# Second layer: the low parts of the turned tiles move from GpSimd to VectorE

## Chip, cores and metric

One NeuronCore of a Trainium2 chip runs the whole kernel in one launch. The metric is device time in microseconds (us), lower is better. Engines in the rows: PE is TensorE, PEld its weight loads, DVE VectorE, ACT ScalarE, POOL GpSimd, SP SyncE (it starts the transfers). PSUM is the memory that PE writes to, SBUF the one that all engines work from.

## What is computed

Two layers over x of shape 8 x 512 x 32 x 32, that is 8 batches of 512 channels by 1024 tokens, all in float32:

```python
# layer 0: group norm, 8 heads of full attention over 1024 tokens, projection, residual
# layer 1 (the change is in here):
q, kk, v = (einsum('oc,bcn->bon', w, xf) for w in (wq, wk, wv))
importance = sum(xf * xf, axis=1)
_, topk_idx = top_k(importance, 256)                 # 256 tokens of each batch
q_sel, k_sel, v_sel = those columns of q, kk, v
q_sel, k_sel = layer_norm(q_sel), layer_norm(k_sel)
attended = softmax(clip(q_sel @ k_sel.T * scale, -80, 80)) @ v_sel
out = v.at[chosen tokens].set(attended)
return x + einsum('oc,bcn->bon', wo, out)
```

## The kernel before

PE multiplies float32 data as pairs: each operand is split into a high part (a copy rounded to the fp32r type) and a low part (the value minus its high part), and a product is high x high + high x low + low x high. So every tile that PE is to read must first be split, one engine writing the high part and another the low one.

The first layer fills the span up to about 2300 us and is not touched. The second handles a batch in four phases, and a *round* i works on four batches at once: t = i + 2 is turned to tokens, its importances are formed and its 256 tokens counted out; a = i + 1 has its chosen rows gathered; b = i is projected to q and k, normed, and attends; c = i - 1 is read back from memory, where the attended rows have been written among its tokens, is turned back to channels and multiplied by the output weights. Only rounds 1 to 8 have a c. In rounds 6 and 7 there is no t any more, in round 8 only c is left. `round_order` (L1104) gives PE's order in a round:

```python
order = [("q", b), ("t", 0, t), ("t", 1, t), ("k", b), ("t", 2, t), ("t", 3, t), ("x", 0, c), ("x", 1, c),
         ("qt", b), ("kt", b), ("rows", t), ("x", 2, c), ("x", 3, c), ("xs", a), ("s", b), ("e", 0, c),
         ("e", 1, c), ("at", b), ("e", 2, c), ("u", b), ("id", t), ("e", 3, c)]
```

`t`: tokens turned (L1281). `q`, `k`: projections (L1356). `x`: a tile of c turned back, 8 transposes into 128 x 1024 of PSUM (L1291). `qt`, `kt`, `xs`: normed q, normed k and the chosen rows turned (L1332). `rows`: importances spread (L1315). `s`: top scores (L1367). `e`: an output tile, 24 matmuls; the first one needs all four split tiles x, a quarter of its matmuls each (L1306). `u`: attended rows (L1389). `id`: sum of the chosen numbers (L1324).

Each of these units writes one of four PSUM slots, dealt out ahead by `tile_slots`. Before PE writes a slot, `free` (L1234) waits for the last reader of the unit that held it. In rounds 2 to 5 `rows` follows x 0 in its slot, x 2 follows x 1, x 3 follows `qt`, `xs` follows `kt`, and `s` follows x 2. In round 8 each e follows the x of its number.

ScalarE goes through the same order: for a turned tile x, `turned_back` (L1458) makes a full float32 copy in SBUF (L1463) and the high part (L1464). GpSimd's `x_low` (L1769) subtracts the two, in SBUF, for all four tiles of the round (L1773); it cannot read PSUM. For `qt`, `kt` and `xs` ScalarE writes the high part (L1485) and VectorE the low one straight from PSUM (`low`, L1600).

VectorE's order in a round stands in the loop at L1689: last output tile of the batch before, layer norm of q and of k (L1607 to L1618), `guard` of the importances, low parts of qt and kt, counts 0 and 1, low part of xs, softmax, counts 2 to 7 among two output tiles, and `choose` (L1564), on whose flags `id` waits. A *count* compares the 1024 importances with 128 of them (L1547, L1549, L1551).

The full copy had no place of its own: its buffer is given up as soon as it is named, and x_low lies on the same addresses, so GpSimd subtracts in place.

Of the kernel before, what the change touches and what calls it, by code (L numbers as in the profile page):

```python
# [8 lines left out]
ALU = mybir.AluOpType  # L9
ACT = mybir.ActivationFunctionType  # L10
F32 = mybir.dt.float32
# [3 lines left out]
P = 128  # L15
# [1078 lines left out]
def batches_of(i):  # L1094


    return [batch(b) for b in (i + 2, i + 1, i, i - 1)]
# [46 lines left out]
def top_layer(nc, x1, y, raw4, ln_wb, shapes_only, ident):  # L1144
# [3 lines left out]
    with first.ctx as ctx:  # L1148
# [3 lines left out]
        def sem(name):  # L1152
            return ctx.enter_context(nc.semaphore(name))
# [30 lines left out]
        fin = flat(qn)[:, 0:RT * TOP].bitcast(U32).rearrange("p (r c) -> p r c", r=RT)  # L1184
        xsel = sb("x_chosen", [P, RT, C])
        xh = sb("x_high", [P, CT, N], F32R)
        with nc.sbuf_tensor("x_back_full", [P, CT, N], F32) as xf:
            pass
        xl = sb("x_low", [P, CT, N], F32R)
        ranks, lower = sb("rank_numbers", [P, TOP]), sb("lower_tokens", [P, P])  # L1190
        equal = sb("equal_flags", [P, P])[:, :].bitcast(BF16).rearrange("p (i x) -> p i x", i=2)
# [8 lines left out]
        xtok = [nc.dram_tensor(f"token_major{i}", [N, C], F32).ap() for i in range(4)]  # L1200

        s_unit, s_load_w = sem("s_unit1"), sem("s_load_w")
        a_tok, a_sq, a_hi, a_ex, a_xf, a_xh, a_row, a_z = (
            sem(n) for n in ("a_tok", "a_sq", "a_hi", "a_ex", "a_xf", "a_xh", "a_row", "a_z"))
        d_imp, d_cnt, d_sel, d_id, d_lo, d_ln, d_sm, d_set, d_row, d_y = (
            sem(n) for n in ("d_imp", "d_cnt", "d_sel", "d_id", "d_lo", "d_ln", "d_sm", "d_set", "d_row", "d_y"))
        p_pow, p_xl = sem("p_pow"), sem("p_xl")
        a_w, d_w, s_wr, a_wqk, p_wqk, s_lnb = (
            sem(n) for n in ("a_w", "d_w", "s_wr", "a_wqk", "p_wqk", "s_lnb"))
        s_gath = [sem(f"s_gath{r}") for r in range(RT)]  # L1210
# [17 lines left out]
        def slot(u):  # L1228
            return ring[:, SLOT1[u], :]

        def second_tensor(pe, last_output):
            mm, tr = nc.tensor.matmul, nc.tensor.transpose

            def free(u):  # L1234

                w = HOLDER1[u]
                if w is None:
                    if SLOT1[u] < 2:
                        pe.wait_ge(told["s_p32"], TILES)
                    elif SLOT1[u] == 2:  # L1240
                        pe.wait_ge(told["s_mx"], 2 * NT * ALL_HEADS)
                        pe.wait_ge(told["s_nd"], 2 * ALL_HEADS)
                    else:
                        pe.wait_ge(told["s_kql"], told["units_read"][0])
                        pe.wait_ge(told["s_vl"], told["units_read"][1])
                else:
                    b = w[-1]
                    if w[0] == "t":
                        pe.wait_ge(a_sq, NT * b + 2 * w[1] + 2)
                    elif w[0] == "w":  # L1250
                        pe.wait_ge(d_w, w[1] + 1)
                    elif w[0] == "o":
                        pe.wait_ge(told["s_x1"], told["residual_done"](w[1]))
                    elif w[0] == "rows":
                        pe.wait_ge(d_cnt, cn((("c", NT - 1), b)))
                    elif w[0] == "id":
                        pe.wait_ge(d_id, ids((1, b)))
                    elif w[0] == "x":
                        pe.wait_ge(a_xh, CT * b + w[1] + 1)
                    elif w[0] == "e":  # L1260
                        pe.wait_ge(d_y, CT * b + w[1] + 1)
                    elif w[0] == "u":
                        pe.wait_ge(a_z, b + 1)
                    elif w[0] in ("q", "k"):
                        pe.wait_ge(d_ln, ln((w[0], "w1", b)))
                    elif w[0] == "s":
                        pe.wait_ge(d_sm, sf(("scale", b)))
                    else:
                        pe.wait_ge(d_lo, lo(w))
                return slot(u)  # L1270
# [24 lines left out]
            def output(u):  # L1295
                _, t, b = u
                out = free(u)
                pe.wait_ge(a_w, 2)
                pe.wait_ge(d_w, 2)
                for c in range(CT):  # L1300
                    if t == 0:
                        pe.wait_ge(a_xh, CT * b + c + 1)
                        pe.wait_ge(p_xl, CT * b + c + 1)
                    for i, (a, w) in enumerate(((0, xh), (0, xl), (1, xh))):
                        for n in range(2):
                            done = mm(out[:, n * HALF:(n + 1) * HALF], ww[a][:, c, t * P:(t + 1) * P],  # L1306
                                      w[:, c, n * HALF:(n + 1) * HALF], start=(c == 0 and i == 0),
                                      stop=(c == CT - 1 and i == 2))
                done.then_inc(s_unit, 1)
# [126 lines left out]
        def second_scalar(act, last_o_high):  # L1436
# [21 lines left out]
            def turned_back(u):  # L1458
                _, c, b = u
                act.wait_ge(s_unit, unit(u))  # L1460
                if b > 0:
                    act.wait_ge(s_unit, unit(("e", CT - 1, b - 1)))
                act_(xf[:, c, :], slot(u), ACT.Copy).then_inc(a_xf, 1)  # L1463
                act_(xh[:, c, :], slot(u), ACT.Copy).then_inc(a_xh, 1)  # L1464

            def rows_high(b):
# [57 lines left out]
        def second_vector(dve, last_o_low, last_residual):  # L1524
# [56 lines left out]
            def rows_low(b):  # L1581
                dve.wait_ge(a_row, b + 1)
                v.tensor_tensor(flat(xrow[1][:, :, :]), flat(xsel[:, :, :]), flat(xrow[0][:, :, :]).bitcast(F32),
                                ALU.subtract).then_inc(d_row, 1)

            def y_tile(t, b):
                u, m = ("e", t, b), CT * b + t
                dve.wait_ge(s_unit, unit(u))
                dve.wait_ge(s_again[t % 2], 16 * (2 * b + t // 2 + 1))
                if m > 1:  # L1590
                    dve.wait_ge(s_out[m % 2], 16 * (m // 2))
                else:
                    for c in range(CT):
                        dve.wait_ge(*told["stored"](BATCH - 1, c))
                v.tensor_tensor(ys[:, m % 2, :], slot(u), xr[:, t % 2, :], ALU.add).then_inc(d_y, 1)
# [93 lines left out]
            for i in ROUNDS[2:]:  # L1689
# [14 lines left out]
                    layer_norm("k", b)  # L1704
                if t is not None:
                    guard(t)
                if b is not None and i > 0:
                    low(("qt", b))
                    low(("kt", b))
                if t is not None:  # L1710
                    for n in range(2):
                        count(t, n)
                if a is not None:
                    low(("xs", a))
                if b is not None:
# [24 lines left out]
        def second_gpsimd(pool):  # L1740
# [25 lines left out]
                    nc.gpsimd.indirect_dma_start(xtok[b % 4], bass.IndirectOffsetOnAxis(idx[:, b % 3, r:r + 1], 0),  # L1766
                                                 changed[b % 2][:, r, :], None).then_inc(s_scat[r], 16)

            def x_low(b):  # L1769
                for c in range(CT):  # L1770
                    pool.wait_ge(a_xf, CT * b + c + 1)
                    pool.wait_ge(a_xh, CT * b + c + 1)
                    nc.gpsimd.tensor_tensor(xl[:, c, :], xf[:, c, :], xh[:, c, :].bitcast(F32),  # L1773
                                            ALU.subtract).then_inc(p_xl, 1)

            def weights_low(i):
                row = (wq_row, wk_row)[i]
                pool.wait_ge(a_wqk, i + 1)
# [4 lines left out]
            weights_low(0)  # L1783
            weights_low(1)
            for i in ROUNDS:
                _, a, b, c = batches_of(i)
                if a is not None:
                    gather(a)
                if i == -1:
                    rstd("q", a)  # L1790
                    rstd("k", a)
                elif b is not None and i > 0:
                    rstd("q", b)
                    rstd("k", b)
                if c is not None:
                    x_low(c)
                if b is not None:
                    scatter(b)

# [201 lines left out]
```

## Time and profile before

| | |
|---|---|
| median of 3 runs | 2801.49 us (2796.53 to 2802.63) |
| profiled execution, its own time | 2800.42 us |
| its span | 2798.7 us |
| PE busy | 2640.9 us, 94% |
| VectorE busy | 2068.8 us, 74% |
| ScalarE busy | 1599.2 us, 57% |
| GpSimd busy | 318.9 us, 11% |
| granted clock of PE, mean | 0.984 |

The share of busy time is a mean over the whole program. The round lengths, from one projection of q to the next, are about 56 us in rounds 2 to 5, 54 in round 6, 52 in round 7 and 44 for the rest. "Idle before" in a row of the timeline is the time for which the engine stood still before the instruction, with the one that released it.

### The profile page before, as it was taken

The page shows a single profiled execution, that of the slowest core. Times are in us where ns is not written, and L with a number is a line of the kernel's source. Part 1 is how long each engine was busy: PE and PEld are TensorE (multiplying, and loading weights), DVE is VectorE, ACT ScalarE, POOL GpSimd, SP SyncE. Part 2 cuts the span into 40 slices and gives each one's busy share as a digit, 9 for nine tenths or more (in the row PEclk, how much of TensorE's full clock was granted, in tenths as well). Part 3 has the DMA queues.
Part 4 walks back from the last instruction along what each step waited for, and adds up shares of the span by engine and source line. Part 5 has one row for each costly group of instructions (what it writes and reads, how often), then busy time and mean ns, then how long its engine had stood idle before and what let it go on. Part 6 is the DMA issues. An engine that isn't in the chain of part 4 may idle for free.

```text
span 2798.7 us, 33246 instructions
## 1 busy us (share of the span) xinstructions
PE 2640.9 (94%) x11856; PEld 2195.8 (78%) x11856; DVE 2068.8 (74%) x3262; ACT 1599.2 (57%) x1962; POOL 318.9 (11%) x166
## 2 busy tenths in 40 slices
PE   6999999999999999999999999999999975899987
PEld 5778887888888888888888888888888764787776
DVE  6888768876887688778877887788777756677652
ACT  3767646764676467646755675567556732533331
POOL 1001001000000000000000000001000121322222
PEclk9999999999999999999999999999999997999999
DMA  4522241214122312131213221322222253645534
GB/s 159 169 57 76 56 126 47 80 54 125 50 76 62 120 46 87 54 117 49 85 53 117 57 79 51 119 56 80 65 83 80 75 211 139 222 166 203 192 110 143
DMA packets 154850, 279.48 MB, mean 100 GB/s; under 512 B 51776, under 2 KB 52032, under 8 KB 154176
## 3 DMA queue, kind: packets, MB, share of 16 engines
q1 hardware_dynamic: 152128, 268.98, 30.5%
q0 software_dynamic: 2560, 8.39, 0.9%
q8 instruction: 96, 1.57, 0.2%
q14 instruction: 66, 0.54, 0.1%
HBM read 180.04 MB, written 63.18 MB: 87 GB/s over the span
## 4 chain that ended last, share of the span: by engine, by line
PE 76%; DVE 15%; issue 3%; ACT 3%; DMA 2%; SPq 1%; POOL 0%; POOLq 0%; DVEq 0%; ACTq 0%
PE tiles L371 8%; PE tiles L372 8%; PE tiles L373 8%; PE tiles L427 8%; PE tiles L473 7%; PE tiles L450 7%; PE tiles L467 7%; PE tiles L466 7%; PE tiles L446 7%; DVE p_low L695 4%; PE tiles L1306 3%; PE tiles L1356 3%; DVE row_max L679 2%; DVE flags L1547 1%; DVE flags L1549 1%
## 5 line engine op out<-in xcount | busy, mean ns | idle before, releaser
L679 DVE TENSOR_REDUCE row_max<-tiles 128x1 f32<-128x512 f32 x1014 | 695.1, 686 | 421.2 <-PE tiles L427 416.6
L543 ACT ACTIVATE p_high<-tiles 128x1024 fp32r<-128x1024 f32 x512 | 525.8, 1027 | 616.7 <-PE tiles L450 615.9
L695 DVE TENSOR_TENSOR p_low<-p_full,p_high 128x1024 fp32r<-128x1024 f32 x512 | 663.1, 1295 | 6.0 <-ACT p_full L546 5.2
L546 ACT ACTIVATE p_full<-tiles 128x1024 f32<-128x1024 f32 x512 | 521.8, 1019 | 0.0
L427 PE MATMUL tiles<-k_high_low,q_high_high 128*128 128x512 f32 x1014 | 409.9, 404 | 7.6 <-DVE row_max L679 6.9
L466 PE MATMUL tiles<-p_high,v_high 128*128 128x512 f32 x1024 | 406.9, 397 | 2.2 <-ACT num_den L562 1.3
L467 PE MATMUL tiles<-p_high,v_low 128*128 128x512 f32 x1024 | 402.5, 393 | 0.0
L878 POOL TENSOR_TENSOR o_normed<-num_den,o_normed 64x1024 f32<-64x1024 f32 x64 | 165.4, 2584 | 2050.8 <-DMA o_normed<-rec_rows 2050.8
L427 PEld LDWEIGHTS tiles<-k_high_low,q_high_high 128*128 128x128 f32 x1014 | 313.1, 309 | 63.3 <-DVE row_max L679 21.7
L473 PE MATMUL tiles<-p_low,v_high 128*128 128x512 f32 x1024 | 326.5, 401 | 16.1 <-DVE p_low L695 15.7
L450 PE MATMUL tiles<-q_low_max,k_high_one 65*128 65x512 f32 x1024 | 325.6, 399 | 1.0 <-DMA q_low_max<-row_max_top 1.0
L371 PE MATMUL tiles<-h_high,w_high 128*128 128x512 f32 x768 | 305.2, 397 | 18.6 <-DVE row_max L679 9.3
L446 PE MATMUL tiles<-q_high_high,k_high_low 128*128 128x512 f32 x1024 | 317.2, 391 | 0.0
L372 PE MATMUL tiles<-h_low,w_high 128*128 128x512 f32 x768 | 302.1, 393 | 0.0
L373 PE MATMUL tiles<-h_high,w_low 128*128 128x512 f32 x768 | 300.9, 392 | 0.0
L446 PEld LDWEIGHTS tiles<-q_high_high,k_high_low 128*128 128x128 f32 x1024 | 192.4, 188 | 47.0
L450 PEld LDWEIGHTS tiles<-q_low_max,k_high_one 65*128 65x128 f32 x1024 | 193.8, 190 | 43.5 <-DMA q_low_max<-row_max_top 2.0
L473 PEld LDWEIGHTS tiles<-p_low,v_high 128*128 128x128 f32 x1024 | 190.1, 189 | 47.3 <-DVE p_low L695 27.8
L466 PEld LDWEIGHTS tiles<-p_high,v_high 128*128 128x128 f32 x1024 | 192.9, 188 | 38.2 <-ACT num_den L562 2.1
L467 PEld LDWEIGHTS tiles<-p_high,v_low 128*128 128x128 f32 x1024 | 192.6, 188 | 38.0
L371 PEld LDWEIGHTS tiles<-h_high,w_high 128*128 128x128 f32 x768 | 146.1, 190 | 45.0 <-issue 25.2
L373 PEld LDWEIGHTS tiles<-h_high,w_low 128*128 128x128 f32 x768 | 145.4, 189 | 32.3
(168 smaller groups left out, 3259.7 us busy)
## 6 DMA issues: line engine op xcount, KB each, us to landing
x_tiles<-in_x SPq DMA_DIRECT2D x64, 512.0 KB, 5.3
w_high<-w_split SPq DMA_DIRECT2D x126, 256.0 KB, 2.8
w_low<-w_split SPq DMA_DIRECT2D x126, 256.0 KB, 2.9
k_high_one<-k_high_low SPq DMA_DIRECT2D x128, 128.0 KB, 2.3
q_high_high<-q_high_high SPq DMA_DIRECT2D x128, 128.0 KB, 2.3
o_normed<-rec_rows SPq DMA_DIRECT2D x64, 256.0 KB, 3.7
x<-x_tiles SPq DMA_DIRECT2D x32, 512.0 KB, 4.0
x_full<-x SPq DMA_DIRECT2D x32, 512.0 KB, 6.0
```

What stands on the lines that cost most here:

```text
L371: mm(fill[:, :], w1, high[:, c, cols], start=(c == 0), stop=False)
L372: mm(fill[:, :], w1, low[:, c, cols], start=False, stop=False)
L373: last = mm(fill[:, :], w2, high[:, c, cols], start=False, stop=(c == CT - 1))
L427: mm(max_bank(h, i, n)[:, :], q1[:, q_slot(h), first:first + HALF - 3:4], k1[:, k_slot(h), n * HALF:(n + 1) * HALF], start=True, stop=True ...
L446: mm(out[:, n * HALF:(n + 1) * HALF], k1[:, wk, keys[n]], q1[:, wq, queries], start=True, stop=False)
L450: last = mm(out[:, n * HALF:(n + 1) * HALF], k2[0:HD + 1, wk, keys[n]], q2[0:HD + 1, wq, queries], start=False, stop=True)
L466: mm(pv[:, :], weights_of(v1, t, n), p, start=(t % 4 == 0 and n == 0), stop=False)
L467: last = mm(pv[:, :], weights_of(v2, t, n), p, start=False, stop=False)
L473: last = mm(pv[:, :], weights_of(v1, t, n), pl[:, t % 2, n * HALF:(n + 1) * HALF], start=False, stop=(t % 4 == 3 and n == 1))
L543: nc.scalar.activation(ph[:, r, :], ring[:, r, :], ACT.Exp, scale=ATT_SCALE).then_inc(s_ph, 1)
L679: nc.vector.reduce_max(mcol[:, h % 2, n, i:i + 1], max_bank(h, i, n)[:, :], AX_X).then_inc(s_mx, 1)
L695: tt(pl[:, r, :], p32[:, r, :], ph[:, r, :].bitcast(F32), ALU.subtract).then_inc(s_pl, 1)
```

## The change

VectorE takes the low part of each turned tile from its PSUM slot, as it does for q, k and the chosen rows. ScalarE writes only the high part, GpSimd has no part in it, and the full copy goes. A slot with a turned tile is now free when its low part is done, not when its high part is. In VectorE's order the first two low parts stand ahead of those of q and k, the other two between counts 0 and 1.

```diff
@@ top_layer, allocation and semaphores
         xh = sb("x_high", [P, CT, N], F32R)
-        with nc.sbuf_tensor("x_back_full", [P, CT, N], F32) as xf:
-            pass
         xl = sb("x_low", [P, CT, N], F32R)
...
-        a_tok, a_sq, a_hi, a_ex, a_xf, a_xh, a_row, a_z = (
-            sem(n) for n in ("a_tok", "a_sq", "a_hi", "a_ex", "a_xf", "a_xh", "a_row", "a_z"))
+        a_tok, a_sq, a_hi, a_ex, a_xh, a_row, a_z = (
+            sem(n) for n in ("a_tok", "a_sq", "a_hi", "a_ex", "a_xh", "a_row", "a_z"))
...
-        p_pow, p_xl = sem("p_pow"), sem("p_xl")
+        p_pow, d_xl = sem("p_pow"), sem("d_xl")
@@ second_tensor, free
                     elif w[0] == "x":
-                        pe.wait_ge(a_xh, CT * b + w[1] + 1)
+                        pe.wait_ge(d_xl, CT * b + w[1] + 1)
@@ second_tensor, output
                     if t == 0:
                         pe.wait_ge(a_xh, CT * b + c + 1)
-                        pe.wait_ge(p_xl, CT * b + c + 1)
+                        pe.wait_ge(d_xl, CT * b + c + 1)
@@ second_scalar, turned_back
-                act_(xf[:, c, :], slot(u), ACT.Copy).then_inc(a_xf, 1)
                 act_(xh[:, c, :], slot(u), ACT.Copy).then_inc(a_xh, 1)
@@ second_vector
+            def x_low(c, b):
+                dve.wait_ge(a_xh, CT * b + c + 1)
+                v.tensor_tensor(xl[:, c, :], slot(("x", c, b)), xh[:, c, :].bitcast(F32), ALU.subtract).then_inc(d_xl, 1)
...
                 if t is not None:
                     guard(t)
+                if c is not None:
+                    x_low(0, c)
+                    x_low(1, c)
                 if b is not None and i > 0:
                     low(("qt", b))
                     low(("kt", b))
                 if t is not None:
-                    for n in range(2):
-                        count(t, n)
+                    count(t, 0)
+                if c is not None:
+                    x_low(2, c)
+                    x_low(3, c)
+                if t is not None:
+                    count(t, 1)
                 if a is not None:
                     low(("xs", a))
@@ second_gpsimd
-            def x_low(b):
-                for c in range(CT):
-                    pool.wait_ge(a_xf, CT * b + c + 1)
-                    pool.wait_ge(a_xh, CT * b + c + 1)
-                    nc.gpsimd.tensor_tensor(xl[:, c, :], xf[:, c, :], xh[:, c, :].bitcast(F32),
-                                            ALU.subtract).then_inc(p_xl, 1)
...
-                _, a, b, c = batches_of(i)
+                _, a, b, _ = batches_of(i)
...
-                if c is not None:
-                    x_low(c)
                 if b is not None:
                     scatter(b)
```

VectorE in round 2 (the same in 1 to 5), from the end of `guard` to the low part of the chosen rows; before:

```order
L1536 COPY_PREDICATED importance<-importance_finite,importance 128x8
L1600 TENSOR_TENSOR q_turned_parts<-tiles,q_turned_parts 128x1024
L1600 TENSOR_TENSOR k_turned_parts<-tiles,k_turned_parts 128x1024
L1549 TENSOR_SCALAR flags,counts<-tiles,importance 128x1024
L1551 SCALAR_TENSOR_TENSOR equal_flags,counts<-tiles,importance,lower_tokens 128x128
L1547 TENSOR_SCALAR flags,counts<-tiles,importance 128x128
L1549 TENSOR_SCALAR flags,counts<-tiles,importance 128x896
L1551 SCALAR_TENSOR_TENSOR equal_flags,counts<-tiles,importance,lower_tokens 128x128
L1600 TENSOR_TENSOR x_chosen_parts<-tiles,x_chosen_parts 128x1024
```

and now, where L1585 is `x_low`, L1601 `low`, and L1544 to L1548 are the counts:

```order
L1533 COPY_PREDICATED importance<-importance_finite,importance 128x8
L1585 TENSOR_TENSOR x_low<-tiles,x_high 128x1024 x2
L1601 TENSOR_TENSOR q_turned_parts<-tiles,q_turned_parts 128x1024
L1601 TENSOR_TENSOR k_turned_parts<-tiles,k_turned_parts 128x1024
L1546 TENSOR_SCALAR flags,counts<-tiles,importance 128x1024
L1548 SCALAR_TENSOR_TENSOR equal_flags,counts<-tiles,importance,lower_tokens 128x128
L1585 TENSOR_TENSOR x_low<-tiles,x_high 128x1024 x2
L1544 TENSOR_SCALAR flags,counts<-tiles,importance 128x128
L1546 TENSOR_SCALAR flags,counts<-tiles,importance 128x896
L1548 SCALAR_TENSOR_TENSOR equal_flags,counts<-tiles,importance,lower_tokens 128x128
L1601 TENSOR_TENSOR x_chosen_parts<-tiles,x_chosen_parts 128x1024
```

Two passes over 128 x 1024 have come in ahead of the low parts of q and k, and two ahead of the second count.

ScalarE in the same place, its order from the last tile turned to tokens on; before:

```order
L1463 ACTIVATE x_back_full<-tiles 128x1024
L1464 ACTIVATE x_high<-tiles 128x1024
L1463 ACTIVATE x_back_full<-tiles 128x1024
L1464 ACTIVATE x_high<-tiles 128x1024
L1485 ACTIVATE q_turned_parts<-tiles 128x1024
L1485 ACTIVATE k_turned_parts<-tiles 128x1024
L1463 ACTIVATE x_back_full<-tiles 128x1024
L1464 ACTIVATE x_high<-tiles 128x1024
L1463 ACTIVATE x_back_full<-tiles 128x1024
L1464 ACTIVATE x_high<-tiles 128x1024
L1485 ACTIVATE x_chosen_parts<-tiles 128x1024
```

and now:

```order
L1461 ACTIVATE x_high<-tiles 128x1024 x2
L1482 ACTIVATE q_turned_parts<-tiles 128x1024
L1482 ACTIVATE k_turned_parts<-tiles 128x1024
L1461 ACTIVATE x_high<-tiles 128x1024 x2
L1482 ACTIVATE x_chosen_parts<-tiles 128x1024
```

Four passes over 128 x 1024 have gone; the high parts stand in the same order as before. On GpSimd the only thing gone from a round is x_low, which stood between the powers of the layer norm and the scatter.

## Rows read from the trace of the kernel before

**Rows 1.** Waits between engines, 2370 to 2799 us: engine line waited for: us, times, longest
```profile
PE tiles L1324 <- DVE chosen L1564: 2.7, 5, 0.7
```
**Rows 2.** Chain of waits, round 4: start us, us, what
```profile
2563.61 0.92 ACT x_chosen_parts L1485
...
2564.56 1.23 DVE x_chosen_parts L1600
...
2586.91 5.59 PE tiles L1306 x24
```
**Rows 3.** Timeline of ACT, round 4: start us, us, operation xcount [idle before <-releaser]
```profile
2554.37 1.01 ACT L1463 ACTIVATE x_back_full<-tiles 128x1024 f32<-128x1024 f32 x1
2555.28 1.02 ACT L1464 ACTIVATE x_high<-tiles 128x1024 fp32r<-128x1024 f32 x1
```
**Rows 4.** Timeline of DVE, round 4
```profile
2554.90 0.17 DVE L1536 COPY_PREDICATED importance<-importance_finite,importance 128x8 f32<-128x8 uint32 x1
2559.07 1.23 DVE L1600 TENSOR_TENSOR q_turned_parts<-tiles,q_turned_parts 128x1024 fp32r<-128x1024 f32 x1 [4.01 <-ACT q_turned_parts L1485]
...
2561.35 1.27 DVE L1549 TENSOR_SCALAR_CACHE_REDUCE flags<-tiles,importance 128x1024 bf16<-128x1024 f32 x1
...
2562.82 0.34 DVE L1547 TENSOR_SCALAR_CACHE_REDUCE flags<-tiles,importance 128x128 bf16<-128x128 f32 x1
...
2564.43 0.08 DVE L1551 DVE_READ_ACCUMULATOR equal_flags<-tiles,importance,lower_tokens 128x1 f32 x1
...
2565.70 0.68 DVE L1625 TENSOR_SCALAR q_k_normed<-tiles 128x512 f32<-128x512 f32 x1
```
**Rows 5.** Timeline of PE, round 4: top scores, and the sum of the chosen numbers
```profile
2562.40 3.12 PE L1367 MATMUL tiles<-k_turned_parts,q_turned_parts 128*128 128x256 f32 x24
...
2585.72 1.19 PE L1324 MATMUL tiles<-chosen,token_numbers 128*128 128x256 f32 x8 [0.64 <-DVE chosen L1564]
```
**Rows 6.** Timeline of DVE, round 1; then the line L1627, all: ns min/median/max
```profile
2388.76 1.22 DVE L1600 TENSOR_TENSOR q_turned_parts<-tiles,q_turned_parts 128x1024 fp32r<-128x1024 f32 x1 [4.01 <-ACT q_turned_parts L1485]
...
2394.66 1.22 DVE L1600 TENSOR_TENSOR x_chosen_parts<-tiles,x_chosen_parts 128x1024 fp32r<-128x1024 f32 x1 [0.47 <-ACT x_chosen_parts L1485]
...
2396.52 0.83 DVE L1627 TENSOR_SCALAR q_k_normed<-q_k_normed 128x512 uint32<-128x512 f32 x1
...
L1627 DVE TENSOR_SCALAR q_k_normed<-q_k_normed x8: 426/548/2214, 2345.9 to 2730.4; 128x512 uint32<-128x512 f32 x8
```
**Rows 7.** Windows, in round 3 and round 4 whole: PE, PEld, DVE, ACT, POOL busy, PEclk, DMA
```profile
2503.00:2508.00 5.00, 4.86 (x28) 4.86 (x29) 4.30 (x12) 4.42 (x5) 4.03 (x3) 0.66 0.26 104
...
2536.00:2592.00 56.00, 51.69 (x289) 43.65 (x288) 39.93 (x107) 22.76 (x38) 15.53 (x11) 1.00 0.59 206
```
**Rows 8.** Round 6: timelines of DVE, POOL and PE, in this order
```profile
2657.74 0.75 DVE L1618 SCALAR_TENSOR_TENSOR q_k_normed<-q_k_normed,ln_rstd,ln_weight_bias 128x512 f32<-128x512 f32 x1
...
2663.36 2.11 DVE L1618 SCALAR_TENSOR_TENSOR q_k_normed<-q_k_normed,ln_rstd,ln_weight_bias 128x512 f32<-128x512 f32 x1
...
2662.57 5.10 POOL L1773 TENSOR_TENSOR x_low<-x_back_full,x_high 128x1024 fp32r<-128x1024 f32 x2
...
2668.28 1.97 PE L1332 MATMUL tiles<-identity,q_k_normed 128*128 128x128 f32 x8 [6.08 <-DVE q_k_normed L1618]
...
2674.41 3.11 PE L1367 MATMUL tiles<-k_turned_parts,q_turned_parts 128*128 128x256 f32 x24
```
**Rows 9.** Round 7: timeline of PE
```profile
2722.10 1.97 PE L1332 MATMUL tiles<-identity,q_k_normed 128*128 128x128 f32 x8 [6.07 <-DVE q_k_normed L1618]
...
2726.53 3.11 PE L1367 MATMUL tiles<-k_turned_parts,q_turned_parts 128*128 128x256 f32 x24 [0.20 <-DVE k_turned_parts L1600]
```
**Rows 10.** Round 8: timelines of POOL and PE
```profile
2766.85 9.37 POOL L1773 TENSOR_TENSOR x_low<-x_back_full,x_high 128x1024 fp32r<-128x1024 f32 x4 [14.01 <-ACT x_high L1464]
...
2769.43 0.70 PE L1306 MATMUL tiles<-x_high,w_part 128*128 128x512 f32 x2
...
2776.36 0.70 PE L1306 MATMUL tiles<-x_high,w_part 128*128 128x512 f32 x2 [0.74 <-POOL x_low L1773]
```

## The prediction

> **What bounds the kernel now.** The change touches only the second layer's rounds 1 to 8, the last 420 us of the span. I read them in this order: the waits between engines, the chain of waits of one round, then the timelines of the engines at the places where the edits stand.
>
> Two kinds of stop lie on the path. PE's sum of the chosen numbers waits for VectorE's flags in each of five rounds [rows 1], 0.64 us in round 4 [rows 5]: once the turned tiles are split, VectorE paces rounds 1 to 5. And twice PE stands 6.1 us for VectorE's layer norm of k, in rounds 6 and 7 [rows 8, 9].
>
> The chain of round 4 [rows 2] shows who paces the stretch before. ScalarE is on it until 2564.53, with its copy of the chosen rows; VectorE starts their low part at 2564.56 and from there to the flags it has no idle time worth naming. Ahead of that VectorE had stood 4.01 us for ScalarE [rows 4]. So in rounds 1 to 5 ScalarE's four full copies lie on the path, and VectorE has a hole about as large as the work that it is to get.
>
> **The change, part by part.**
>
> *Full copies gone (ScalarE).* 32 copies go, four to a round; ScalarE starts one every 0.91 us [rows 3], so 3.6 us a round.
>
> *Low parts come to VectorE.* Its nearest relatives are the low parts of q and k, also PSUM minus SBUF over 128x1024: they last 1.23 us and start 1.14 apart (2559.07 to 2561.35 is two of them) [rows 4]. I take 1.14 for each in a row and 1.23 for the last. No row speaks for less, so the lower end is rival C, that the hole swallows them whole; the upper is 1.27, the VectorE pass over 1024 elements beside it. The value follows the nearest row. Four to a round at 1.14 is 4.56 us.
>
> *Rounds 1 to 5, worked on round 4.* ScalarE is free for the turned tiles at 2554.37. Its first high part now ends at 2555.39, so the first low part starts at 2555.42; VectorE was ready at 2555.07 and waits 0.35. From there it has work without a stop: two low parts, low q, low k, first count 1.47 (2561.35 to 2562.82), two low parts, second count 1.61 (2562.82 to 2564.43), low part of the chosen rows: 7 x 1.14 + 3.08 = 11.06, so it comes to the softmax at 2566.48. Before: 2565.70 [rows 4]. That is 0.78 late. What each of these waits for is ready: the second pair of turned tiles is written once the second low part has released its slot (2557.79), and low q (2558.93); eight PE instructions of this size take at most the 1.19 of [rows 5], which puts the ends of ScalarE's third and fourth high parts at about 2560.1 and 2561.2, ahead of 2561.45 and 2562.59; the chosen rows' high part, behind low k's release at 2560.07, ends at 2562.4, ahead of 2565.34.
>
> PE's new wait is the one with people behind it: the top scores take the slot of the third turned tile, so they start when its low part has ended, 2561.45 + 1.23 = 2562.68. They started at 2562.40 [rows 5], so PE is 0.35 late with the release; the outputs are queued behind. The scores last 3.12 and end before 2566.48, and PE had 0.64 of slack before the flags, so VectorE's 0.78 is what counts.
>
> GpSimd's work goes, and with it a slowdown: the check for finite scores takes 0.55 in the median and took 0.83 in round 1, where its shortest instance is 0.43 [rows 6]. That gives back 0.12, and 0.40 in round 1. Rounds 2 to 5: 0.66 each, 2.64 in all. In round 3 the clock fell for a while (0.66 granted [rows 7]) and the old kernel was late by itself; I price it as the others.
>
> Round 1 differs: q's tile is turned late there, so low q, at 2388.76 before [rows 6], cannot come much earlier; I take 2388.5. Then low k, count, two low parts, count; the low part of the chosen rows starts at 2388.5 + 2 x 1.14 + 1.47 + 2 x 1.14 + 1.61 = 2396.1, against 2394.66 [rows 6]: 1.45 late, less 0.40: 1.05.
>
> *Round 6.* No counting here. The second step of the layer norm takes 0.75 when alone and 2.11 beside GpSimd's low parts, which run from 2662.57 to 2667.67 [rows 8]; the second of k's pair lasts 2.05. So the layer norm of k ends 1.36 + 1.30 = 2.66 earlier, and PE's turn of k starts at 2665.62, not 2668.28. Behind the layer norm VectorE now has two low parts, low q and low k (4 x 1.14, ended by 2670.1). PE's own row of k, two turned tiles and the chosen rows took from 2668.28 to 2674.41 [rows 8], 6.13 us; shifted, the scores start at 2671.75. The releases (first low part 2666.7, second 2667.9, low k 2670.1) are all in time. Gain 2.66.
>
> *Round 7.* The same pair of stretched steps, 2.66 us; the turn of k moves from 2722.10 [rows 9] to 2719.44. But the scores waited for low k, and three new or moved passes stand ahead of that on VectorE: from 2719.31, 3 x 1.14 + 1.23 ends at 2723.96, so the scores start at 2724.05 instead of 2726.53: gain 2.48.
>
> *Round 8.* Nothing but the last four turned tiles and their output. GpSimd takes 9.37 us for four low parts, and PE's first output starts at 2769.43 and comes to its last quarter at 2776.36, having waited three times [rows 10]. Eighteen matmuls at the pace of the chain's row, 5.59 / 24 = 0.233 [rows 2], need 4.19. ScalarE's high parts now follow the turning itself, the last one ends near 2770.8 and its low part near 2772.1; the last quarter needs it at 2773.6. Gain 6.93 - 4.19 = 2.74; everything after it is PE without a stop.
>
> *Sum:* 1.05 + 2.64 - 2.66 - 2.48 - 2.74 = -4.2 us. Against the profiled execution (2800.42) that is 2796.2; the median of the runs shown, 2801.49, stands 1.07 above it, so I predict 2797.3. One run to another this kernel differs by up to 6 us, and 0.2%, 5.6 us, is about what a measurement can tell from no change; the forecast lies inside.
>
> **The rivals.**
>
> *A. The clock stays up in round 6, and the gain passes the threshold.* PE's turn of k took 1.97 for 8 transposes after 6.08 us of idle [rows 8], against 1.19 for 8 larger matmuls [rows 5]. Its stop shrinks by 2.66, to 3.4 us. If the clock holds, the scores wait only for low k (2670.1) instead of PE (2671.75): 1.7 us more. The sum is -5.9: 2795.6. For it: the shorter gap. Against it: round 7 has one like it and is bound by VectorE then.
>
> *B. PE's clock falls in the steady rounds; slower than before.* PE now stands 1.5 us in one piece ahead of the scores (chosen rows turned by about 2561.2, scores at 2562.75), where before its idle time was cut up. In round 3 the clock fell in just this stretch [rows 7]. If the scores run at the lower level, 3.12 becomes about 6.2; they then end at 2569, 2.5 us after VectorE needs them. In one round that eats more than half the gain, in two the kernel is level, and in all five it is 12.5 - 4.2 = +8.3: 2809.8. It decides from two rounds on. For it: the clock did fall in round 3. Against it: round 4 kept 1.00 from end to end [rows 7] with short stops in the same place, and the new pause replaces those.
>
> The Trainium skill bears on B ("TensorE: Matmul & The Clock Gate", What's actually happening): the reduced clock is the default and only activity lifts it, so a longer pause speaks for a fall. By that rule alone the sum would be that of B; the trace bears it out in part, as the one round shows a fall and the other none.
>
> *C. The hole on VectorE is not paid for.* If VectorE's new passes and the chain that ScalarE leaves come out even, rounds 1 to 5 cost nothing and only the gains stand: -7.9, 2793.6. For it: the hole was 4.01 and the passes are 4.56. Against it: VectorE cannot start them before ScalarE's first high part.
>
> *D. Rounds 6 and 7 don't gain.* If GpSimd was not what stretched the layer norm, only round 8 gains: 1.05 + 2.64 - 2.74 = +1.0, 2802.5. Against it: the same step lasts 0.75 in the same round before GpSimd starts [rows 8].
>
> **How the numbers follow.** Forecast, whose own range is 2794.5 to 2800: 0.47, a tenth of it beyond the threshold. A, 0.24; C, 0.09 (both faster by over 0.2%; with that tenth 0.37). D, 0.06, no change. B in up to four rounds, 0.07, no change; in five, or with D, 0.07, slower. Faster 0.37, same 0.56 (0.43 + 0.06 + 0.07), slower 0.07. The range takes in C below (2793.6 less 2 for the runs' own spread) and D with the upper price of the pass (5 rounds x 4 x 0.13 = 2.6, with 2801.49 + 1.0 = 2802.5 rounded): 2791.5 to 2804.5.
>
> **What would show it.** Right: VectorE has no 4 us gap before low q in rounds 1 to 5; it comes to the softmax 0.8 later counted from ScalarE's last square; the round from one q projection to the next is 0.7 longer; the layer norm's steps of k all last 0.75 in rounds 6 and 7 and PE's stop there is 3.4 instead of 6.1; in round 8 the first output has no stop. Wrong: low parts over 1.3 us on VectorE, a granted clock under 1 at the scores, an output of a steady round waiting for a low part, or scores in round 7 that still wait for something other than low k.

## The result, and the profile after

The kernel after takes 2793.8 us (12 runs, 2783.74 to 2799.93), the kernel before 2799.9 on the same chip (12 runs, 2796.53 to 2803.16). The ratio is 0.9976, with a 95% interval of 0.9966 to 0.9987: by the ratio 6.7 us faster (3.6 to 9.5; the two medians stand 6.1 apart). The forecast was 4.2 us and 2797.3. The interval holds the 4.2, and 2793.8 lies in the stated range (2791.5 to 2804.5), though just under what I had called the forecast's own (2794.5 to 2800); 6.7 is 0.24%, just past the 0.2% under which I had put the likeliest case.

The profiled execution took 2791.04 us, its span is 2789.2. The page's first part:

```profile
span 2789.2 us, 33182 instructions
PE 2639.5 (95%) x11856; PEld 2192.5 (79%) x11856; DVE 2103.8 (75%) x3294; ACT 1571.9 (56%) x1930; POOL 239.1 (9%) x134
```

VectorE has 35 us more work, ScalarE 27 less, GpSimd 80 less, PE the same: what was moved arrived.

*The steady rounds.* The timeline of round 4 after, from ScalarE's first high part of a turned tile to VectorE's softmax. Columns as before: start, length, engine, line, operation, what it writes and reads, count, idle time before with its releaser. ScalarE and then VectorE:

```profile
2553.32 1.93 ACT L1461 ACTIVATE x_high<-tiles 128x1024 fp32r<-128x1024 f32 x2
```

```profile
2554.37 2.36 DVE L1585 TENSOR_TENSOR x_low<-tiles,x_high 128x1024 fp32r<-128x1024 f32 x2 [0.37 <-ACT x_high L1461]
2556.64 1.21 DVE L1601 TENSOR_TENSOR q_turned_parts<-tiles,q_turned_parts 128x1024 fp32r<-128x1024 f32 x1
...
2560.38 2.35 DVE L1585 TENSOR_TENSOR x_low<-tiles,x_high 128x1024 fp32r<-128x1024 f32 x2
...
2564.25 1.22 DVE L1601 TENSOR_TENSOR x_chosen_parts<-tiles,x_chosen_parts 128x1024 fp32r<-128x1024 f32 x1
2565.39 0.68 DVE L1626 TENSOR_SCALAR q_k_normed<-tiles 128x512 f32<-128x512 f32 x1
```

The 4.01 us gap of [rows 4] is gone, two low parts in a row start 1.14 us apart and the last lasts 1.21 to 1.22. From the start of ScalarE's first pass over a turned tile, now a high part, to the softmax are 12.07 us (2553.32 to 2565.39); the prediction had 12.11 (2554.37 to 2566.48). Before, where that first pass was a full copy, it was 11.33 [rows 3, 4]. PE in the same round:

```profile
2555.65 1.09 PE L1313 MATMUL tiles<-identity,importance 128*128 128x128 f32 x8 [0.66 <-DVE x_low L1585]
...
2561.65 3.13 PE L1365 MATMUL tiles<-k_turned_parts,q_turned_parts 128*128 128x256 f32 x24 [1.45 <-DVE x_low L1585]
...
2585.30 1.17 PE L1322 MATMUL tiles<-chosen,token_numbers 128*128 128x256 f32 x8 [0.95 <-DVE chosen L1561]
```

It stands 1.45 us ahead of the scores, which last 3.13 as against 3.12 [rows 5], so at the higher clock level (granted 1.00, as everywhere from 2404 to 2660); and 0.95 ahead of the sum of the chosen numbers, where it stood 0.64.

*Rounds 6 and 7.* First all instances of the layer norm's second step and of the check for finite scores, grouped by line (shortest, median and longest in ns, first and last start):

```profile
L1619 DVE SCALAR_TENSOR_TENSOR q_k_normed<-q_k_normed,ln_rstd,ln_weight_bias x32: 751/752/754, 2295.3 to 2715.2; 128x512 f32<-128x512 f32 x32
L1628 DVE TENSOR_SCALAR q_k_normed<-q_k_normed x8: 426/426/428, 2343.8 to 2724.5; 128x512 uint32<-128x512 f32 x8
```

None is stretched any more; before, the longest were 2.11 us of the one [rows 8] and 2.21 of the other [rows 6]. PE in round 6, then in round 7:

```profile
2665.80 1.72 PE L1330 MATMUL tiles<-identity,q_k_normed 128*128 128x128 f32 x8 [3.42 <-DVE q_k_normed L1619]
2667.31 3.00 PE L1289 MATMUL tiles<-identity,x_back 128*128 128x128 f32 x16
...
2670.93 3.12 PE L1365 MATMUL tiles<-k_turned_parts,q_turned_parts 128*128 128x256 f32 x24
...
2715.97 1.09 PE L1330 MATMUL tiles<-identity,q_k_normed 128*128 128x128 f32 x8 [3.41 <-DVE q_k_normed L1619]
...
2720.59 3.17 PE L1365 MATMUL tiles<-k_turned_parts,q_turned_parts 128*128 128x256 f32 x24
```

PE stands 3.4 us for the layer norm of k, where it stood 6.1 [rows 8, 9]. In round 7 VectorE's low part of k starts at 2719.23 and lasts 1.22, and the scores start 0.14 behind its end, at 2720.59. But PE did not stand still for it: in both rounds its clock fell soon after the turn of k had begun, and in round 7 the turned tiles ran at the lower level nearly up to the scores. PE's windows there: length, busy time, granted clock, and what the DMA moved:

```profile
2666.10:2669.50 3.40, 3.40 (x19) 0.50 0.00 0
2669.60:2674.00 4.40, 4.40 (x40) 1.00 0.01 4
2717.30:2720.60 3.30, 3.30 (x17) 0.50 0.00 0
```

*Round 8*, PE and the last three low parts:

```profile
2757.97 5.07 PE L1289 MATMUL tiles<-identity,x_back 128*128 128x128 f32 x28 [2.31 <-DMA x_back<-token_major]
2762.79 0.71 PE L1304 MATMUL tiles<-x_high,w_part 128*128 128x512 f32 x2
```

```profile
2761.88 3.73 DVE L1585 TENSOR_TENSOR x_low<-tiles,x_high 128x1024 fp32r<-128x1024 f32 x3 [0.48 <-ACT x_high L1461]
```

The stops of [rows 10] are gone, and the first output follows the turning without one.

*Where the time went, by rounds.* A round is read off PE's timeline, from the first matmul of its q projection to the next one. All kernels of the study, in us ("end of r8" is from the start of the first output to the end of the span; the names are those of the experiments below):

| kernel | r1 | r2 | r3 | r4 | r5 | r6 | r7 to end | end of r8 |
|---|---|---|---|---|---|---|---|---|
| before | 58.91 | 56.21 | 57.24 | 56.17 | 56.19 | 53.83 | 96.34 | 29.27 |
| before, looked at again | 58.94 | 56.15 | 56.22 | 56.21 | 56.22 | 52.91 | 97.14 | 29.27 |
| after | 59.79 | 56.79 | 56.84 | 56.83 | 56.80 | 50.17 | 90.31 | 26.41 |
| after, looked at again | 59.99 | 56.80 | 56.81 | 56.79 | 56.81 | 50.04 | 90.05 | 26.49 |
| rounds 6 to 8 only | 58.97 | 56.19 | 56.18 | 56.19 | 56.19 | 50.08 | 90.06 | 26.40 |
| rounds 1 to 5 only | 59.99 | 56.80 | 56.81 | 56.82 | 56.81 | 52.87 | 97.09 | 29.33 |
| GpSimd waits | 58.94 | 56.21 | 57.21 | 56.18 | 56.23 | 50.16 | 94.86 | 29.37 |
| mixed | 58.89 | 55.33 | 55.32 | 55.30 | 55.30 | 50.10 | 90.06 | 26.39 |
| mixed, last pair | 60.59 | 58.17 | 58.20 | 58.20 | 58.15 | 50.17 | 90.06 | 26.35 |
| copies kept | 61.06 | 58.64 | 59.25 | 58.63 | 58.65 | 50.17 | 91.42 | 27.34 |

The table is the instrument of this study: a round repeats to some 0.05 us from kernel to kernel when nothing in it was changed, apart from 0.6 to 1.0 more in round 3 of three of them (before, GpSimd waits, copies kept), while whole executions of one kernel spread over up to 16 us. In those three rounds the granted clock was 0.50 for some 3 us ahead of the scores; in the kernel before from 2503.1 to 2506.5. Part of that spread lies ahead of the change: q of round 1 starts anywhere from 2360.6 to 2368.9 in these ten profiles, whatever is edited behind it.

### The profile page after: what moved, and what is told of

Read it like the earlier page. It is cut to its first block, busy times and chain, and to the rows that moved or that the text cites. A ratio compares the mean times of both kernels' runs of the same rounds, so it can differ in the third digit from the quotient of the medians.

```text
span 2789.2 us, 33182 instructions
## 1 busy us (share of the span) xinstructions
PE 2639.5 (95%) x11856; PEld 2192.5 (79%) x11856; DVE 2103.8 (75%) x3294; ACT 1571.9 (56%) x1930; POOL 239.1 (9%) x134
## 4 chain that ended last, share of the span: by engine, by line
PE 76%; DVE 15%; issue 4%; DMA 2%; ACT 1%; SPq 1%; POOL 0%; DVEq 0%; POOLq 0%; ACTq 0%
PE tiles L371 8%; PE tiles L372 8%; PE tiles L427 8%; PE tiles L373 8%; PE tiles L473 7%; PE tiles L450 7%; PE tiles L466 7%; PE tiles L467 7%; PE tiles L446 7%; DVE p_low L695 4%; PE tiles L1304 4%; DVE row_max L679 2%; PE tiles L1354 2%; DVE flags L1546 1%; DVE flags L1544 1%
```

## The experiments

Most kernels are the changed one with a rule for who takes a low part. Where it says GpSimd, ScalarE writes the full copy as well, and the slot is free with the high part, as before:

```diff
+        def by_vector(c, b):          # tile c of batch b; b is the round less 1
+            return ...
@@ free
-                        pe.wait_ge(d_xl, CT * b + w[1] + 1)
+                        if by_vector(w[1], b):
+                            pe.wait_ge(*low_done(w[1], b))
+                        else:
+                            pe.wait_ge(a_xh, CT * b + w[1] + 1)
@@ turned_back
+                if not by_vector(c, b):
+                    act_(xf[:, c, :], slot(u), ACT.Copy).then_inc(a_xf, 1)
```

**Only rounds 6 to 8.**

```diff
+            return b >= 5
```

> VectorE takes the low parts only in rounds 6 to 8; rounds 1 to 5 are those of the kernel before (full copy on ScalarE, low part on GpSimd). Theory (a sum over rounds: 1 to 5 lose 0.6 to 0.9 us each, 6 to 8 gain 2.66 + 2.48 + 2.74): the loss goes and the gain stays, -7.9 us against the kernel before, rounds 1 to 5 as long as before, 56.2 us from one q projection to the next. Rival (the gain comes from GpSimd's leaving the rounds 1 to 5, or from something outside the second layer): only what is left of the gain in rounds 6 to 8, less than -4 us. If in addition the shorter stops of PE keep its clock up in rounds 6 and 8, up to 2 us more, -10.

Measured (12 runs): 2790.17 against 2801.09, ratio 0.9963 [0.9952, 0.9974], -10.4 us (-13.4 to -7.3). The late rounds carry all of the gain; rounds 1 to 5 are those of the kernel before. By the table the gain over the second trace of before is 2.8 in round 6 and 7.1 from there to the end, 9.9. I had expected 7.9, and 10 only if PE's clock stayed up. It did not: granted 0.50 from 2662.4 to 2665.8 in round 6 and from 2713.6 to 2717.0 in round 7. Where the 2 us come from is told below, under round 7 and round 8.

**Only rounds 1 to 5.**

```diff
+            return b < 5
```

> The other half: VectorE takes the low parts only in rounds 1 to 5, rounds 6 to 8 are those of the kernel before. Theory: slower, +3.7 us against the kernel before (1.05 in round 1, 0.66 in each of 2 to 5), with layer norm steps of 2.1 us beside GpSimd's low parts in rounds 6 and 7 as before. Rival (early rounds gain too): at or below 0.

Measured (12 runs): 2804.28, ratio 1.0016 [1.0003, 1.0029], +4.5 us (0.8 to 8.1). So the move costs time in the rounds in which VectorE also counts. Rounds 6 to 8 are those of the kernel before, stretched steps included:

```profile
L1638 DVE SCALAR_TENSOR_TENSOR q_k_normed<-q_k_normed,ln_rstd,ln_weight_bias x32: 750/752/2109, 2300.0 to 2723.6; 128x512 f32<-128x512 f32 x32
```

**GpSimd waits.** All low parts stay with GpSimd; in rounds 6 and 7 it waits for the end of the layer norm of k before it takes the first.

```diff
+            return False
@@ second_gpsimd, ahead of the low parts of a round
+                if i in (6, 7):
+                    pool.wait_ge(d_ln, ln(("k", "b1", i)))
```

> The kernel before with one wait more: in rounds 6 and 7 GpSimd starts its four low parts only when VectorE has finished the layer norm of k. Theory (GpSimd stretches the layer norm's second step from 0.75 to 2.1): all such steps take 0.75, PE's stop for the turn of k falls from 6.1 to 3.4 us in both rounds, and GpSimd's 9.5 us of low parts still end before the output needs the last one: -2.7 in round 6, -2.7 in round 7, none in round 8, -5.3 in all. Rival (it is not GpSimd but the layer norm's own place that costs): steps of 2.1 remain, 0; or the late low parts make the output wait: above -3.

Measured (12 runs): 2792.62, ratio 0.9974 [0.9963, 0.9986], -7.3 us (-10.4 to -3.9). By the table, against the second trace of before, it is 2.75 in round 6 and 2.3 from there to the end, 5.0, where I had expected 5.3. The steps of the layer norm by line, then GpSimd and PE in round 6:

```profile
L1638 DVE SCALAR_TENSOR_TENSOR q_k_normed<-q_k_normed,ln_rstd,ln_weight_bias x32: 750/752/754, 2303.7 to 2719.7; 128x512 f32<-128x512 f32 x32
```

```profile
2670.40 9.40 POOL L1803 TENSOR_TENSOR x_low<-x_back_full,x_high 128x1024 fp32r<-128x1024 f32 x4 [3.10 <-DVE q_k_normed L1638]
```

```profile
2670.38 1.09 PE L1345 MATMUL tiles<-identity,q_k_normed 128*128 128x128 f32 x8 [3.43 <-DVE q_k_normed L1638]
...
2675.51 3.11 PE L1380 MATMUL tiles<-k_turned_parts,q_turned_parts 128*128 128x256 f32 x24
```

GpSimd does all its work, only later, and round 6 is as short as in the changed kernel (50.16 against 50.17). What the layer norm suffered from was GpSimd's work at the same time, not the number of passes on any engine. In round 7 the scores start 22.12 us after q, where they start 24.17 and 24.77 after it in the two traces of before. Round 8, which has no layer norm, keeps its stops (29.37). Here the trace bears out the Trainium skill ("SBUF — State Buffer", SBUF: two separate sides): a VectorE instruction that reads two SBUF operands and a GpSimd instruction that reads SBUF exclude each other for the whole instruction. The step takes two SBUF operands, and it lasted 2.1 us beside a GpSimd pass of 2.35 and 0.75 without one.

**Mixed.** In rounds 1 to 5 VectorE takes the first two tiles and GpSimd the last two, in the rest VectorE takes all.

```diff
+            return b >= 5 or c < 2
```

> In rounds 1 to 5 VectorE takes the low parts of turned tiles 0 and 1 alone, and tiles 2 and 3 keep the full copy and GpSimd; in rounds 6 to 8 VectorE takes all. Theory (VectorE has a hole of 4 us ahead of low q, none behind it, and ScalarE paces the stretch): two passes of 1.14 fit into the hole and ScalarE is two copies shorter, so VectorE comes to the softmax about 0.9 us earlier than in the kernel before; rounds 2 to 5 are 0.9 shorter each, round 1 even, rounds 6 to 8 gain 7.9: -11.5 us against the kernel before. Rival (VectorE's passes in these rounds cost what they last): +2.3 a round instead, about +3 in all.

Measured (6 runs): 2783.68, ratio 0.9945 [0.9927, 0.9963], -15.4 us (-20.4 to -10.4). It beats both kernels, and its steady rounds are shorter than either's by 0.9 and 1.5 us. ScalarE, VectorE and GpSimd in round 4:

```profile
2548.44 1.93 ACT L1478 ACTIVATE x_high<-tiles 128x1024 fp32r<-128x1024 f32 x2
```

```profile
2549.49 2.36 DVE L1604 TENSOR_TENSOR x_low<-tiles,x_high 128x1024 fp32r<-128x1024 f32 x2 [0.36 <-ACT x_high L1478]
...
2557.75 1.22 DVE L1620 TENSOR_TENSOR x_chosen_parts<-tiles,x_chosen_parts 128x1024 fp32r<-128x1024 f32 x1 [0.56 <-ACT x_chosen_parts L1499]
2558.89 0.68 DVE L1645 TENSOR_SCALAR q_k_normed<-tiles 128x512 f32<-128x512 f32 x1
```

```profile
2555.11 4.77 POOL L1801 TENSOR_TENSOR x_low<-x_back_full,x_high 128x1024 fp32r<-128x1024 f32 x2 [9.32 <-ACT x_high L1478]
```

From the start of ScalarE's first pass over a turned tile to the softmax are 10.45 us (2548.44 to 2558.89), against 11.33 before and 12.07 after. VectorE's hole of 4 us is filled with two passes and ScalarE is rid of the two copies that made it; the other two low parts, which would have pushed VectorE past ScalarE, stay with the idle engine. VectorE's own low part at 2557.75 lasts 1.22 beside GpSimd's pass, as it does alone; one of its operands is in PSUM. The whole gained 4 us more than the 11.5 that I had expected: 2 of them are those of the late rounds above, the rest is inside the interval of six runs.

**Mixed, last pair.** The same shares, the other way round: GpSimd the first two tiles, VectorE the last two.

```diff
+            return b >= 5 or c > 1
```

> As the mixed version, but in rounds 1 to 5 VectorE takes the low parts of turned tiles 2 and 3, and tiles 0 and 1 keep the full copy and GpSimd: as many passes and copies on each engine as there, in another place. Theory (only VectorE's time ahead of low q is free): low q starts where it did in the kernel before, the two passes come on top, and the third and fourth high parts are not earlier where it counts: VectorE comes to the softmax 2.15 us later than before, rounds 2 to 5 last 58.3 us instead of 56.2 (mixed: 55.3); with the 10 us that rounds 6 to 8 gave alone the whole is level with the kernel before. Rival (what counts is the number of passes and copies): rounds of 55.3 as in the mixed version.

Measured (10 runs): 2800.38 against 2799.73, ratio 1.0002 [0.9990, 1.0013]. A steady round is 2.9 us longer than with the other pair, at equal work for each engine. ScalarE and VectorE in round 4:

```profile
2555.94 1.02 ACT L1477 ACTIVATE x_back_full<-tiles 128x1024 f32<-128x1024 f32 x1
```

```profile
2560.64 1.22 DVE L1620 TENSOR_TENSOR q_turned_parts<-tiles,q_turned_parts 128x1024 fp32r<-128x1024 f32 x1 [4.02 <-ACT q_turned_parts L1499]
...
2564.38 2.35 DVE L1604 TENSOR_TENSOR x_low<-tiles,x_high 128x1024 fp32r<-128x1024 f32 x2
...
2569.39 0.68 DVE L1645 TENSOR_SCALAR q_k_normed<-tiles 128x512 f32<-128x512 f32 x1
```

The full copies now stand ahead of q's high part, so VectorE keeps its hole of 4.02 us and gets two passes behind it: 13.45 us from ScalarE's first copy to the softmax (2555.94 to 2569.39). PE's clock is not the cause: it was low for 3.4 us ahead of the scores in rounds 3, 4 and 5 of this trace (2562.2 to 2565.6 in round 4) and 1.00 all through round 2, and the four rounds are equally long.

**Copies kept.** The changed kernel, but ScalarE still makes the full copies, which nobody reads.

```diff
@@ turned_back
+                act_(xf[:, c, :], slot(u), ACT.Copy)
```

> The changed kernel with ScalarE's full copies left in; nothing reads them any more. Theory (dropping the copies is what nearly pays for VectorE's passes in rounds 1 to 5): the first low part starts 0.9 us later, and the chain of high parts keeps VectorE waiting after that; it comes to the softmax about 1.6 us later than in the changed kernel, rounds 2 to 5 last 58.4 us instead of 56.8; rounds 6 and 7 are within 0.5 of the changed kernel. In all about 8 us over the changed kernel, +1 against the kernel before. Rival (ScalarE isn't on the path once VectorE has the low parts): rounds of 56.8.

Measured (10 runs): 2804.83 against 2799.73, ratio 1.0015 [1.0004, 1.0025], +4.2 us (1.1 to 7.0). Round 4:

```profile
2566.06 1.01 ACT L1476 ACTIVATE x_back_full<-tiles 128x1024 f32<-128x1024 f32 x1
```

```profile
2568.02 1.22 DVE L1603 TENSOR_TENSOR x_low<-tiles,x_high 128x1024 fp32r<-128x1024 f32 x1 [1.27 <-ACT x_high L1477]
2569.85 1.22 DVE L1603 TENSOR_TENSOR x_low<-tiles,x_high 128x1024 fp32r<-128x1024 f32 x1 [0.60 <-ACT x_high L1477]
...
2579.94 0.68 DVE L1644 TENSOR_SCALAR q_k_normed<-tiles 128x512 f32<-128x512 f32 x1
```

VectorE waits for ScalarE ahead of each of the first two low parts, 1.27 and 0.60 us, and comes to the softmax 13.88 us after ScalarE's first copy. Dropping the copies is worth 58.64 - 56.80 = 1.84 us in a steady round, moving the low parts costs 58.64 - 56.20 = 2.44: the 0.6 of the change is the difference of these two. In the late rounds the copies cost nothing in round 6 and 1.1 to 1.4 from there on. I had expected a steady round of 58.4 and +1 for the whole. The 8 us over the changed kernel that this rested on are 1.6 in each of five rounds; it was 1.84 in a steady round, 0.6 more in round 3, where the clock fell, and the 1.1 to 1.4 of the late rounds I had left out.

**After, and before, looked at again.** One more profiled execution of each, for what a single trace cannot say of the clock.

> The changed kernel once more, for its rounds alone. Theory (round lengths are fixed by the chain and only PE's clock varies them): rounds 2 to 5 within 0.1 of 56.8 unless the granted clock falls in one of them, then +0.7 to +1.1 there; the scores of round 6 start 22.2 us after q again. Rival (the 1.0 us more in round 6 than forecast was luck of the clock): 23.2.

> The kernel before once more, for its rounds alone: rounds 2, 4 and 5 at 56.2, round 3 at 56.2 or 57.2 by the clock; the scores of round 6 start 25 to 26 us after q, those of round 7 24.2 to 24.8, and the first output of round 8 runs with three stops, 29.3 us from its start to the end of the span.

Measured: 2789.67 and 2799.68. No round from 2 to 5 of the changed kernel is longer than 56.84, and in the ten rounds 1 to 5 of both traces the scores last 3.12 to 3.14, with a granted clock of 1.00 from 2404 to 2660: PE's pause ahead of the scores did not lower the clock. The scores of round 6 start 22.10 us after q, as in the first trace (22.21). In the kernel before, the long round 3 (57.24) did not come back (56.22), so it belongs to single executions and not to every one. But its round 8 starts differently; PE in the second trace, and below it the row of the first that answers:

```profile
2762.89 5.17 PE L1291 MATMUL tiles<-identity,x_back 128*128 128x128 f32 x28 [2.22 <-DMA x_back<-token_major]
2768.63 0.70 PE L1306 MATMUL tiles<-x_high,w_part 128*128 128x512 f32 x2 [0.57 <-POOL x_low L1773]
```

```profile
2763.61 6.06 PE L1291 MATMUL tiles<-identity,x_back 128*128 128x128 f32 x28 [2.18 <-DMA x_back<-token_major]
```

Here PE turns the tiles in 5.17 us and then stands 0.57 for GpSimd's first low part; in the two experiments that leave round 8 as it was before it stands 0.54 (rounds 1 to 5 only) and 0.50 (GpSimd waits). In the first trace the turning took 6.06, since the granted clock was 0.50 up to 2769.4, to its very end, and the stop was hidden in it; in the second it was 0.50 only up to 2766.8.

## Why the prediction was right, and where it was off

*Steady rounds, +0.66 each: right.* +0.61 (56.80 less 56.19, the rounds of the kernel with the late change alone), by the mechanism named: the softmax was to come 12.11 us after the start of ScalarE's first high part, and came 12.07 after it. "Rounds 1 to 5 only" confirms it for the whole kernel, +4.5 against 1.05 + 2.64 = 3.7, and "copies kept" shows both terms by themselves. The new wait before the scores is there (1.45 us, forecast 1.5) and costs nothing of its own: the scores end at 2564.78, ahead of the softmax. Round 1: +0.9 to +1.1, forecast +1.05.

*Round 6, -2.66: right.* -2.8 (52.9 less 50.1) in the usual case. The first pair of traces shows -3.66 (53.83 less 50.17), and 0.9 of that is PE's clock in one execution: after the same stop of 6.1 us, k's turn to the scores took 6.13 in the first trace of before [rows 8] and 5.24 in the second. The granted clock was 0.50 for equally long in both, but it fell 1.3 us ahead of the turn of k in the first (2667.0) and 3.2 ahead of it in the second (2664.4), so there less of PE's work met it:

```profile
2667.58 1.97 PE L1332 MATMUL tiles<-identity,q_k_normed 128*128 128x128 f32 x8 [6.07 <-DVE q_k_normed L1618]
...
2672.82 3.12 PE L1367 MATMUL tiles<-k_turned_parts,q_turned_parts 128*128 128x256 f32 x24
```

*Round 7, -2.48: right by the first trace, too small by the second.* The scores started 24.17 us after q in the first trace of before and start 21.70 after it now: -2.47. In the second trace, and in "rounds 1 to 5 only", the turning behind k ran at the lower clock level to its end and the old scores came at 24.77, so that the gain is 3.07:

```profile
2720.50 1.97 PE L1332 MATMUL tiles<-identity,q_k_normed 128*128 128x128 f32 x8 [6.07 <-DVE q_k_normed L1618]
2722.26 3.62 PE L1291 MATMUL tiles<-identity,x_back 128*128 128x128 f32 x16
2725.53 3.27 PE L1367 MATMUL tiles<-k_turned_parts,q_turned_parts 128*128 128x256 f32 x24
```

That the scores now follow the low part of k fits: they start 0.14 us behind its end in both traces of after and in "rounds 6 to 8 only". But PE's own tiles end at the same moment, so no trace shows PE standing for it.

*Round 8, -2.74: the mis-sized term.* The three stops gave what was forecast: from the start of the first output to the end of the span it is 26.4 instead of 29.3, -2.9. But the step kept the first output's start where [rows 10] has it. In three of the four profiles with the old round 8 that output also waits for GpSimd, and in the second trace of before the turning with its wait takes 5.74 us (2762.89 to 2768.63), where it takes 4.82 now (2757.97 to 2762.79). That is 0.9 more; the term should have been about -3.8. This is the one term of the sum that was wrong in kind: I had taken the start of that output from a single trace, in which no stop stands ahead of it, and there the lower clock stood in its place.

*The sum.* With the usual values +1.0 (round 1), 4 x 0.61, -2.8 (round 6) and -6.9 (from q of round 7 to the end, 97.1 less 90.2) it is -6.3 us, and -6.7 was measured. The 2.1 us that the forecast lacked are 0.9 at the start of round 8's output and 0.2 behind it, 0.6 in round 7, and 0.4 in rounds 1 to 6 together. They carry the result from 0.15% to 0.24%, over the bound of 0.2% (0.22% by this sum), to which I had given 37% against 56% for no change. All of these errors went the same way, and what kept the time inside the range is its width. Against the 2797.3 the measured 2793.8 is 3.5 lower: 1.9 is the difference of the medians (6.1) less the 4.2, and 1.6 comes in because the kernel before came out at 2799.9 and not at the 2801.49 of its first three runs. The range's upper end was added up wrong (2802.5 and 2.6 make 2805.1, not 2804.5); nothing hangs on it.

*The rivals.* A (the clock stays up in round 6): it did not stay up, but it was low for half as long. In both traces of after it was granted 0.50 for 3.4 us in round 6 and again in round 7, where it had been 6.8 in each before. So in round 6 the turn of k still took 1.72 and 1.97, and the scores started 22.1 to 22.2 us after q, where the forecast says 25.88 - 2.66 = 23.2 and A 21.5. Against the second trace of before, where they started 24.97 after q, the shift of 2.66 is nearly all there is. B (the clock falls before the scores): not seen in rounds 2 to 5 of either trace of after; the longer pause, which was to speak for a fall, brought none. C (the hole is not paid for): refuted by "rounds 1 to 5 only". D (rounds 6 and 7 don't gain): refuted by "GpSimd waits", which takes away only the overlap and is as short in round 6 (50.16).

Whether mixed could still be bettered, with GpSimd taking one tile of the four instead of two, was not tried.

## What to carry to other kernels

Before work is moved to fill an engine's hole, see who makes the hole: two tiles whose copies stood ahead of it were worth moving (-0.9 us a round), the other two only lengthened the engine behind it, and the same split the other way round gave 2.9 us a round away. Judge a stretch-wise change stretch by stretch: this one was a loss in five rounds and a larger gain in three, used only in the three it gained 10.4 us instead of 6.7, and with the first two tiles in the other five 15.4. And a stop that one trace of before does not show can be hidden by a lower clock in that one execution; a second trace is cheap.

## What was not expected of the hardware

What a GpSimd pass over SBUF stretched went by where the VectorE instruction's operands lie, not by how much it reads. Stretched were two instructions that read nothing from PSUM: the layer norm's second step over 512 elements, two SBUF operands, from 0.75 to 2.1 us, and the check for finite scores, with a single SBUF operand, from 0.43 to as much as 2.21. Not stretched were two that take one operand from PSUM: the layer norm's first step, 0.74 in the midst of the same GpSimd passes, and a low part over 1024 elements, 1.22 beside GpSimd as without it. From the trace of before, round 6 and then round 7:

```profile
2665.39 0.74 DVE L1615 SCALAR_TENSOR_TENSOR q_k_normed<-tiles,ln_mean_var,ln_weight_bias 128x512 f32<-128x512 f32 x1
2666.17 2.05 DVE L1618 SCALAR_TENSOR_TENSOR q_k_normed<-q_k_normed,ln_rstd,ln_weight_bias 128x512 f32<-128x512 f32 x1
...
2730.41 2.21 DVE L1627 TENSOR_SCALAR q_k_normed<-q_k_normed 128x512 uint32<-128x512 f32 x1
```

PE's clock comes back at no fixed point after the same idle time: after 6.1 us the same 32 matmuls of round 6 took 5.24 or 6.13 us; after 3.4 us it was low for 3.4 us in both rounds of both traces of after, but for 6.8 in round 7 of "GpSimd waits" (2719.5 to 2726.3). Nor does the longest single stop tell whether it falls: at the stops of 1.45 us ahead of the scores it did not, while in "mixed, last pair" it fell in rounds 3 to 5 with no stop over 1.1 us in the 8 us ahead of it.
